# One of the eight mixing sets of an attention unit in fp32, without low halves, and four instead of six low halves of a unit on VectorE

## The reference

```python
q = _rope(split_heads(_conv(_mcl(x, Wq, bq), q_conv_w, q_conv_b, 3)))
k = _rope(split_heads(_conv(_mcl(x, Wk, bk), k_conv_w, k_conv_b, 3)))
v = split_heads(_conv(_mcl(x, Wv, bv), v_conv_w, v_conv_b, 3))
qk = jnp.einsum('bceqd,bcekd->bceqk', q, k) / math.sqrt(h)
a = jax.nn.softmax(qk, axis=-1)
o = jnp.einsum('bceqk,bcekd->bceqd', a, v)
o = o.transpose(0, 1, 3, 2, 4).reshape(b, c, w, h).transpose(0, 1, 3, 2)
return _conv(_mcl(o, Wo, bo), o_conv_w, o_conv_b, 0)
...
x = x + _L0_conv_ref(_gn(x), ...)   # the attention above
x = x + _L1_conv_ref(_gn(x), ...)   # a 3x3 convolution on a sphere, with bilinear samples
```

## Time and profile before

| | |
|---|---|
| median of 3 runs | 1254.0 us (1251.71 to 1257.11) |
| the profiled execution | 1258.79 us, of which 1256.9 us from first to last instruction |
| mean granted TensorE clock | 0.963 of 2.4 GHz |
| busy, share of the span: PE, DVE, ACT, POOL | 86%, 74%, 53%, 69% |
| attention | about 412 to 980 us |
| bytes moved | 159 MB, 127 GB/s over the span |

### The profile page before, as it was taken

One profiled execution on the slowest core, in us unless ns is written; L12 is line 12 of the kernel. 1 busy time (PEld: TensorE's weight loads), 2 busy tenths in 40 slices (PEclk: granted clock), 3 DMA queues, 4 the chain that ended last, 5 costly groups with the idle time before them and its releaser, 6 DMA issues. The chain is left out here.

```text
span 1256.9 us, 26231 instructions
## 1 busy us (share of the span) xinstructions
PE 1079.0 (86%) x10648; PEld 590.9 (47%) x10648; DVE 933.5 (74%) x1225; ACT 663.2 (53%) x1110; POOL 871.2 (69%) x812
## 2 busy tenths in 40 slices
PE   0299999999894699899998999999988589899998
PEld 0177777777673123333333333333333345355553
DVE  3789999999764798788888888888872584544344
ACT  1555555555442066666666666666666223346345
POOL 0467776777583489899998899988999007937900
PEclk9899999999998589999999999999999799899999
DMA  9725244332644555527171736254000599875661
GB/s 305 238 83 161 76 124 116 104 94 67 139 105 99 115 77 126 111 55 116 49 121 35 122 65 114 57 94 81 31 19 18 184 354 299 265 228 155 190 214 54
DMA packets 137759, 159.02 MB, mean 127 GB/s; under 512 B 17852, under 2 KB 85708, under 8 KB 137640
## 3 DMA queue, kind: packets, MB, share of 16 engines
q1 hardware_dynamic: 113448, 119.37, 39.6%
q10 hardware_dynamic: 15648, 28.81, 6.6%
q0 software_dynamic: 8544, 9.18, 2.8%
HBM read 106.48 MB, written 52.89 MB: 127 GB/s over the span
## 5 line engine op out<-in xcount | busy, mean ns | idle before, releaser
L1108 POOL TENSOR_TENSOR a_pl<-a_prob 128x512 bf16<-128x512 f32 x416 | 443.1, 1094 | 37.0 <-ACT a_prob L1059 36.4
L1012 DVE TENSOR_REDUCE a_negmax<-a_row 128x1 f32<-128x512 f32 x512 | 334.1, 706 | 60.4 <-PE a_row L939 59.2
L1059 ACT ACTIVATE a_prob<-a_col 128x512 f32<-128x512 f32 x512 | 292.1, 596 | 147.0 <-PE a_col L960 140.7
L710 POOL TENSOR_TENSOR f_yl<-f_y,f_yh 128x768 bf16<-128x768 f32 x80 | 132.8, 1679 | 95.8 <-ACT f_yh L657 95.8
L657 ACT ACTIVATE f_yh<-f_y 128x768 bf16<-128x768 f32 x80 | 67.4, 844 | 139.1 <-DVE f_y L548 121.2
L1023 DVE TENSOR_TENSOR a_pl<-a_prob 128x512 bf16<-128x512 f32 x96 | 123.3, 1285 | 19.2 <-ACT a_prob L1059 19.2
L450 PE MATMUL f_acc<-f_wh,f_xh 128*32 128x384 bf16 x1280 | 110.9, 335 | 29.8 <-DVE f_wl L538 26.5
L939 PE MATMUL a_row<-k,q 96*128 96x512 bf16 x256 | 106.6, 423 | 22.7 <-PEq L202 14.9
L960 PE MATMUL a_col<-a_q,a_k 98*128 98x512 bf16 x256 | 97.9, 388 | 23.2 <-ACT a_prob L1059 19.3
L960 PE MATMUL a_col<-q,k 98*128 98x512 bf16 x256 | 99.8, 390 | 16.1 <-ACT a_prob L1059 14.7
L714 POOL TENSOR_TENSOR f_straight<-f_straight,f_turned 128x832 f32<-128x832 f32 x40 | 107.0, 2675 | 9.4 <-DVE f_turned L565 9.4
(11 more groups left out here) (156 smaller groups left out, 2189.2 us busy)
## 6 DMA issues: line engine op xcount, KB each, us to landing
X<-b_x ACTq DMA_DIRECT2D x16, 526.0 KB, 8.3
q<-in_x SPq DMA_DIRECT2D x8, 1024.0 KB, 7.7
a_v<-V SPq DMA_DIRECT2D x16, 512.0 KB, 4.4
Z<-a_z ACTq DMA_DIRECT2D x32, 256.0 KB, 3.5
b_z<-Z SPq DMA_DIRECT2D x16, 512.0 KB, 11.0
b_x<-in_x SPq DMA_DIRECT2D x32, 256.0 KB, 10.1
b_res<-X SPq DMA_DIRECT2D x38, 208.0 KB
out<-b_y ACTq DMA_DIRECT2D x38, 208.0 KB
```

What stands on the lines that cost most here:

```text
L710: nc.gpsimd.tensor_tensor(yl[half][n % 2][:], y[half][:], yh[half][n % 2][:], ALU.subtract).then_inc(yl_done, 1)
L1012: nc.vector.reduce_max(negmax[n % PAIR][:, 0, t:t + 1], row[step % ROWS][:], AX.X, negate=True).then_inc(max_done, 1)
L1059: nc.scalar.activation(prob[sets_done % RING][:, t % QUAD, :], col[step % 2][:], ACT.Exp).then_inc(exp_done, 1)
L1108: nc.gpsimd.tensor_tensor(pl[p][:, r, :], prob[p][:, r, :], ph[p][:, r, :], ALU.subtract).then_inc(lo_pool, 1)
```

## The change

Set 5 of the eight of a unit (`WHOLE`) is computed from the fp32 tiles themselves: `prob` by fp32 ones, and `v` by `prob`, four matmuls each in place of twenty in bf16. Its four steps, 20 to 23, need no low halves. It waits for the exps, the other sets wait for the low halves as before. Of the 28 steps that are left every seventh goes to VectorE (6, 13, 24 and 31; before 4, 9, 14, 19, 24 and 29), the other 24 to GpSimd. Since the set reads `v` itself, and not only its halves, a new v may be loaded over it only when all sets of its unit are through: `load_v` waits for `mixed` in place of `v_lo`. With that later release the order of loads on SP's queue is changed too: q and k of both parts come together, v after them, and of the first call only two v are left, so that the v of unit 2 stands behind the loads for the last stage. There are two tiles of ones, in fp32 and in bf16.

```diff
@@ -744,12 +744,12 @@
         RING = 5
         ROWS = 3
-        EVERY = 5
-        DVE_LOWS = STEPS // EVERY
-        POOL_LOWS = STEPS - DVE_LOWS
+        WHOLE = (HEADS // QUAD * QT - 3,)
+        EVERY = 7
...
-        ones = sb("a_ones", [P, DH], BF16)
+        ones = sb("a_ones", [P, DH])
+        ones16 = sb("a_ones16", [P, DH], BF16)
...
@@ -816,17 +816,17 @@
 
             return t // (QUAD * QT) * QUAD + t % QUAD, t % (QUAD * QT) // QUAD
 
-        def low_on_pool(t):
-
-            return t % EVERY != EVERY - 1
+        SPLIT_STEPS = [t for t in range(STEPS) if t // QUAD not in WHOLE]
+        DVE_STEPS = SPLIT_STEPS[EVERY - 1::EVERY]
+        POOL_STEPS = [t for t in SPLIT_STEPS if t not in DVE_STEPS]
 
         def dve_lows(n, g):
 
-            return DVE_LOWS * n + QUAD * (g + 1) // EVERY
+            return len(DVE_STEPS) * n + sum(t < QUAD * (g + 1) for t in DVE_STEPS)
 
         def pool_lows(n, g):
 
-            return STEPS * n + QUAD * (g + 1) - dve_lows(n, g)
+            return len(POOL_STEPS) * n + sum(t < QUAD * (g + 1) for t in POOL_STEPS)
 
 
         SPLIT = STEPS
@@ -850,8 +850,8 @@
         def steps(first, emit):
             return [(STEPS * n + first + t, lambda n=n, t=t: emit(n, t)) for n in range(UNITS) for t in range(STEPS)]
 
-        def lows(first, emit, on_pool):
-            return [(STEPS * n + first + t, lambda n=n, t=t: emit(n, t)) for n in range(UNITS) for t in range(STEPS) if low_on_pool(t) == on_pool]
+        def lows(first, emit, chosen):
+            return [(STEPS * n + first + t, lambda n=n, t=t: emit(n, t)) for n in range(UNITS) for t in chosen]
 
         def sets(first, emit):
             return [(STEPS * n + first + QUAD * g, lambda n=n, g=g: emit(n, g)) for n in range(UNITS) for g in range(SETS)]
@@ -883,7 +883,7 @@
 
             def load_v(n):
                 if n >= 2:
-                    sp.wait_ge(v_lo, n - 1)
+                    sp.wait_ge(mixed, SETS * (n - 1))
                 sp.dma_start(v[n % 2][:], V[entry(n), channel(n)].rearrange("(t p) f -> p t f", p=P)).then_inc(v_in[n % 2], 16)
 
             def load_wo(i, m):
@@ -896,15 +896,18 @@
                 n = PAIR * i
                 if i:
                     load_qk(i, 0, 0)
+                    load_qk(i, 0, 1)
+                    load_v(n - 1)
                 load_v(n)
+                if i == 0:
+                    load_v(n + 1)
+                load_qk(i, 1, 0)
+                load_qk(i, 1, 1)
                 if i:
-                    load_qk(i, 0, 1)
-                load_v(n + 1)
-                load_qk(i, 1, 0)
-                load_v(n + 2)
-                load_qk(i, 1, 1)
+                    load_v(n + 1)
                 load_wo(i, 0)
-                load_v(n + 3)
+                if i:
+                    load_v(n + 2)
                 load_wo(i, 1)
 
             load(0)
@@ -923,8 +926,10 @@
                         sp.dma_start(to[p1:p1 + KR], T["w_sphere"][kx, ky:ky + 1].broadcast_to([KR, C, C])).then_inc(mixing_in, 16)
             sp.dma_start(side[:], T["side"]).then_inc(mixing_in, 16)
             sp.dma_start(centre[:], T["centre"]).then_inc(mixing_in, 16)
+            load_v(CHANNELS)
             for i in range(1, C // CHANNELS):
                 load(i)
+            load_v(UNITS - 1)
             sp.wait_ge(mixing_in, 16 * (KR + 2 + 3 + 9 + 3))
 
         @block.tensor
@@ -963,25 +968,28 @@
             def mix_set(n, g):
                 kt, quad = g % QT, SETS // QT * n + g // QT
                 p = (SETS * n + g) % RING
-                pe.wait_ge(lo_pool, pool_lows(n, g))
-                pe.wait_ge(lo_dve, dve_lows(n, g))
+                if g in WHOLE:
+                    pe.wait_ge(exp_done, STEPS * n + QUAD * (g + 1))
+                else:
+                    pe.wait_ge(lo_pool, pool_lows(n, g))
+                    pe.wait_ge(lo_dve, dve_lows(n, g))
                 if n == g == 0:
-                    pe.wait_ge(ones_set, 1)
+                    pe.wait_ge(ones_set, 2)
                 if kt == 0 and quad:
                     pe.wait_ge(logged, quad)
-                for part in (ph, pl):
+                for part in (prob,) if g in WHOLE else (ph, pl):
                     for r in range(QUAD):
-                        nc.tensor.matmul(weight[r * DH:(r + 1) * DH, :], ones[:], part[p][:, r, :],
-                                         start=kt == 0 and part is ph, stop=kt == QT - 1 and part is pl)
+                        nc.tensor.matmul(weight[r * DH:(r + 1) * DH, :], (ones if part is prob else ones16)[:], part[p][:, r, :],
+                                         start=kt == 0 and part is not pl, stop=kt == QT - 1 and part is not ph)
                 if g == 0:
                     pe.wait_ge(v_lo, n + 1)
                 if kt == 0 and quad:
                     pe.wait_ge(divided, quad)
-                for j, (vv, part) in enumerate(((vh, ph), (vl, ph), (vh, pl))):
+                for j, (vv, part) in enumerate(((v, prob),) if g in WHOLE else ((vh, ph), (vl, ph), (vh, pl))):
                     for r in range(QUAD):
                         h = g // QT * QUAD + r
                         last = nc.tensor.matmul(mix[r * DH:(r + 1) * DH, :], vv[n % 2][:, kt, h * DH:(h + 1) * DH], part[p][:, r, :],
-                                                start=kt == j == 0, stop=kt == QT - 1 and j == 2)
+                                                start=kt == j == 0, stop=kt == QT - 1 and (g in WHOLE or j == 2))
                 last.then_inc(mixed, 1)
 
             def tail(n, j, part):
...
-            pipeline(steps(0, row_max) + units(SPLIT, split_max) + lows(EXP + 1, low_part, False) + quads(KEEP, divide))
+            pipeline(steps(0, row_max) + units(SPLIT, split_max) + lows(EXP + 1, low_part, DVE_STEPS) + quads(KEEP, divide))
...
-            pipeline(units(EXP - 1, v_low) + lows(EXP + 1, low_part, True))
+            pipeline(units(EXP - 1, v_low) + lows(EXP + 1, low_part, POOL_STEPS))
```

More of the change, by code:

```diff
@@ L1007, in _ @@
             nc.vector.memset(ones[:], 1.0).then_inc(ones_set, 1)
+            nc.vector.memset(ones16[:], 1.0).then_inc(ones_set, 1)
             def row_max(n, t):
```

## The result

The changed kernel takes 1265.94 us, median of 4 runs (1262.19 to 1267.62), against 1254.65 us before (1251.71 to 1257.11): a ratio of 1.0087, 95% interval 1.0055 to 1.0119. It is slower, by 11 us (0.9%) and not by the 41 us that were forecast. Six further runs have a median of 1266.14 us, against 1255.55 us for 23 of the kernel before, ratio 1.0088 (1.0067 to 1.011).

What follows compares the result with a forecast made beforehand. TensorE's instruction stream, with short ScalarE latencies, was taken as the pace. The fp32 sets +40.8, last unit +1.3 and loads -1.4 gave +40.7 us on 1254.0, so 1294.7, about 1295 us; range 1260 to 1312.

Steps and rivals of the forecast that it cites:

- The sign: Whole kernel: slower than before by more than the 6 us a measurement can tell, given 0.92.
- the likeliest case: fp32 set in nine steps of 0.43 us, two records at a time; chance 0.72, own range 1283 to 1311 us.
- Its own terms downwards: Likeliest case's lower margin: 6 us for the divide, 1.5 for loads, 5 if semaphores and part of the last step vanish.
- What bounds the kernel: Steady attention: TensorE's instruction stream with short ScalarE latencies sets the pace; relieving GpSimd or VectorE gives only idle time.
- The fp32 set: Set 5 on TensorE: 3.95 us instead of 1.23, +2.72 us per unit, 40.8 us over units 0 to 14.
- four abreast: Rival for set 5: four strips side by side, 1.8 us a set, +7 us in all, 1261 us; chance 0.09.
- Nothing absorbs it: Units 0 to 14: no waiting or ScalarE work hides the longer set 5; all 2.72 us go on the path.
- The last unit: End of attention: GpSimd done earlier, but set 5 delays sets 6 and 7, +1.3 us instead of 2.7.
- The loads: SP's queue: unit 2's jam goes, -2.9 us; unit 0's maxima delayed 1.5 (0 to 3.5); together -1.4 us.
- the relief at 0: Fewer low halves, 2.2 us less on GpSimd and 2.6 on VectorE per unit: worth zero in the steady part.

Runs made afterwards that it cites:

- the relief alone: Changed kernel with set 5 in bf16 from high halves only, its four steps still without low halves: 1253.62 us, ratio 0.9997 to the kernel before.
- the bf16 kernel with held loads: Kernel before with new load order, side and centre late, second half of q/k held until the first col matmul: 1251.78 us, ratio 0.996.
- the two held kernels: Kernel before and changed kernel, both with new load order, late tables, second half of q/k held until first col matmul: 1251.78 (bf16) and 1259.22 us (fp32).
- the loads alone: Kernel before with only the new order of loads and v released by the sets, all sets bf16: 1257.87 us, ratio 1.0018.
- change again: The changed kernel measured again without edit, in more rounds: 1266.14 against 1255.55 us for the kernel before, ratio 1.0088.

## Why the prediction was wrong

The sign was right. The time lies in the range, but only because the range was drawn down to a rival with a chance of 0.09; the likeliest case, with 1283 us as its lower end, was not the one that came. (Its own terms downwards, 6, 1.5 and 5 us, give 1282.)

- *What bounds the kernel* held. TensorE's stream sets the pace and GpSimd and VectorE have only idle time to gain: the relief alone left a unit at 33.23 us. It did not hold in unit 0, as the sum at the end of this section shows.
- *The fp32 set*, the term that failed: 2.72 us forecast, 0.63 us measured, over 15 units 41 us and 9 us. That an fp32 matmul is two records of 0.43 us was right. The wrong step was "the first record of strip 1 stands behind that one in the queue, and starts with it". In the rows at hand, strips never repeated within a group, so program order and order within a strip could not be told apart; the prediction said so and still took the order of the queue. The two runs with another order of the same matmuls showed that strips are served apart. The lower bound, taken as the rival "four abreast" with 0.09, came true for the set. Its 1261 us are within 5 us of the time, while it too carried the loads at -1.4 us.
- Two pages of the Trainium skill were weighed. "TensorEngine Tiling (Array Packing)", Key Properties, says that tiles operate independently, and the trace agrees: 1.86 us for the fp32 set instead of 3.95. "TensorE: Matmul & The Clock Gate", Part 3, has matmuls start in strict program order, and across strips the traces contradict it: a bf16 set written strip by strip took 1.24 us, where that order would give 2.9 (an estimate, 13 steps of 0.22 us).
- *Nothing absorbs it* held: 0.63 us more on TensorE were 0.63 us more per unit, and a second fp32 set as much again.
- *The last unit*, +1.3 us forecast, did not come. From its last col matmul to the last output matmul it took 11.2 us in the changed kernel and 13.6 before, but the bf16 kernel with held loads took 11.1 too. The kernel before had a granted clock of 0.5 there from 976.7 to 980.1 us, and its first output part took 3.68 us where that of the changed kernel took 2.05 for the same 16 records. So the 2.4 us are no gain of fp32; between the two held kernels the whole stretch from the first col matmul of unit 15 on, with two fp32 sets in it, differs by 0.2 us.
- *The loads*: -2.9 us for unit 2 came as said. For unit 0, 1.5 us were taken and 3.5 the bound; the traces show 2.7 to 5.4. The cause named, `side` and `centre`, was wrong: with both issued long afterwards the wait stayed at 5.4 us with fp32, and holding back half of q and k, with all that stands behind it, took the whole wait away. The step that failed: the new order was read for what it no longer holds back, without asking what the old wait had been keeping off the DMA engines at that moment. With -1.4 us forecast, the loads alone were measured at +2.3 us (interval -0.4 to +5), +3.4 in the trace.

The traces let the whole difference be added up, from the first col matmul of one unit to that of the next. The fp32 set of a unit stands behind the first col matmul of the next, so the stretch of unit 0 has none, and that of unit 15 has two. All in us, rounded:

| stretch | change again, less before | held loads: fp32 less bf16 |
|---|---|---|
| first row matmul to first col matmul | +5.6 | 0.0 |
| unit 0 | -2.2 | -1.7 |
| units 1 and 2 | -1.6 | +1.2 |
| units 3 to 14 | +7.1 | +7.2 |
| unit 15, to the last output matmul | -0.2 | +0.2 |
| attention | +8.7 | +7.0 |

The left column holds the jam that came (+5.6) and the one that went (-2.9, in units 1 and 2). The right one is the price of fp32 alone: 14 sets at 0.63 us are 8.8, less 0.35 us in unit 7, which lasts 33.5 to 33.6 us in every kernel with six low halves on VectorE and three row tiles, and is as long as its neighbours in the relieved ones, and less 1.7 us in unit 0. There the relief did pay. In both held kernels the granted clock rose to 1.00 at 444.5 us, so the clock is not the reason, but TensorE's weight loads for row scores waited less for VectorE's maxima, first in bf16 (440.89 to 469.86 us), then with fp32 (441.13 to 468.37 us):

```profile
PEld a_row L946 <- DVE a_negmax L1019: 6.2, 12, 0.8
```

```profile
PEld a_row L946 <- DVE a_negmax L1023: 1.8, 4, 0.8
```

The relief alone shows the same against the loads alone, 1.0 us in unit 0. The prediction took the relief at 0 from the steady units and did not look at unit 0 by itself.

What stays open: 1.9 of the 10.6 us between the medians, which these traces do not place, and why unit 0 hangs on VectorE where later units do not. And the trade of the change, a low half less for 0.63 us of TensorE, was only tried where TensorE sets the pace.

## What to carry to other kernels

Before a sum is built on an order within a queue, look whether the rows at hand can tell that order from a weaker one; if they cannot, the cheap bound deserves as much weight as the dear one. When a wait in a DMA queue goes, ask what it had kept out of the way of the small, urgent transfers on other queues: here it was worth nearly as much as all fp32 sets together (6.9 and 7.4 us), and with a single deliberate wait in the new order of loads the bf16 kernel became faster than before the change. Work taken from engines that idle already is no gain, whatever their share; but look for single stretches, as unit 0 here, in which the engine ahead does wait for them.

## What the runs showed of the hardware

- A matmul of one strip of 32 columns starts past waiting matmuls of other strips: twenty bf16 matmuls written strip by strip took five steps of 0.22 to 0.24 us, sixteen fp32 records four steps of 0.43 to 0.45 us, in both written orders that were tried.
- Four fp32 matmuls of 128x32 by 128x512 side by side take 0.88 us. Two such groups cost 1.86 us up to the next matmul, where five groups in bf16 cost 1.23.
- From the issue of a DMA of 16 KB on ScalarE's queue to the matmul that needs it, it took 5.7 to 8.5 us in eight traces in which 3 MB and small loads had been issued in one go on SP's queue, and 2.9 us in the four with free DMA engines. TensorE waited 2.7 to 5.4 us for it.
